# Reordering the small products and one pair of evictions in the first stage of a filtered-convolution and spectral kernel

## The reference

```python
# layer 0: group norm, 2x upsampling FIR in rows and columns, leaky ReLU, 2x downsampling FIR
y = conv(gn(x), up, rows); y = conv(y, up, columns)
y = where(y >= 0, y, 0.01 * y)
y = conv(y, down, rows);   y = conv(y, down, columns)
x = x + y
# layer 1: group norm, 2-D real FFT, a low-rank contraction on 64 x 64 modes (two corners), inverse FFT
x_ft = rfft2(gn(x))
out = contract(x_ft, a, b, c, d)
x = x + irfft2(out)
```

## Time and profile before

| what | us |
|---|---|
| median of 3 runs (lowest to highest) | 4960.16 (4957.18 to 4960.85) |
| the profiled execution | 4952.49 |
| its span, first to last instruction | 4950.7 |
| PE busy in the span | 4650.8 (94%) |
| DVE busy | 3450.2 (70%) |
| ACT busy | 3279.4 (66%) |
| POOL busy | 3176.7 (64%) |
| first and last x1b<-ring on DVE (line 796), of 256 | 47.9 and 2643.5 |

### The profile page before, as it was taken

How to read it: one execution, slowest core, us unless ns; L and a number is a source line. 1 busy time by engine, 2 the same in 40 slices (tenths; PEclk the granted TensorE clock), 3 DMA queues, 4 the chain that set the end, 5 groups by cost and what they waited for, 6 DMA issues and landing times. The chain is left out here.

```text
span 4950.7 us, 244841 instructions
## 1 busy us (share of the span) xinstructions
PE 4650.8 (94%) x102182; PEld 3998.5 (81%) x102182; DVE 3450.2 (70%) x5227; ACT 3279.4 (66%) x5782; POOL 3176.7 (64%) x3334
## 2 busy tenths in 40 slices
PE   7999999999999999999997599999999999999999
PEld 6887888888878888888886477777777777779999
DVE  5776777777777677767776777777777777773333
ACT  6767767767677677677773577777777777762332
POOL 6867858858678588577681477777777777760000
PEclk9999999999999999999998799999999999999999
DMA  2132132231321321322324122222222222229999
GB/s 61 56 103 71 56 112 62 58 116 57 90 85 57 107 67 56 108 65 74 100 58 159 41 83 78 78 85 80 81 75 85 80 85 72 85 68 398 420 421 398
DMA packets 609975, 556.27 MB, mean 112 GB/s; under 512 B 16996, under 2 KB 543332, under 8 KB 592612
## 3 DMA queue, kind: packets, MB, share of 16 engines
q1 hardware_dynamic: 609380, 547.21, 33.5%
HBM read 278.71 MB, written 268.44 MB: 111 GB/s over the span
## 5 line engine op out<-in xcount | busy, mean ns | idle before, releaser
L1328 DVE TENSOR_TENSOR Ml<-ring,Mh 128x1024 f16<-128x1024 f32 x832 | 982.3, 1219 | 331.0 <-ACT Mh L1291 325.4
L1291 ACT ACTIVATE Mh<-ring 128x1024 f16<-128x1024 f32 x832 | 810.9, 1024 | 336.5 <-PE ring L1217 336.2
L269 POOL TENSOR_TENSOR A<-Af,A 128x788 f16<-128x788 f32 x512 | 862.7, 1685 | 41.4
L754 DVE SCALAR_TENSOR_TENSOR Y<-ring,Y 128x532 f16<-128x532 f32 x1024 | 682.2, 706 | 279.5 <-ACT Y L607 278.9
L1217 PE MATMUL ring<-wcur,b_hi 64*128 64x128 f16 x16384 | 737.4, 217 | 43.9 <-POOL wcur L1156 39.2
L607 ACT ACTIVATE Y<-ring 128x532 f16<-128x532 f32 x1024 | 575.1, 610 | 270.1 <-PE ring L369 257.1
L1217 PEld LDWEIGHTS ring<-wcur,b_hi 64*128 64x128 f16 x16384 | 614.8, 94 | 146.8 <-DVE Ml L1328 100.7
L1217 PE MATMUL ring<-wcur,b_lo 64*128 64x128 f16 x8192 | 711.6, 217 | 0.0
L369 PE MATMUL ring<-uth,A 64*128 64x138 f16 x12288 | 605.0, 223 | 62.0 <-issue 29.4
L267 POOL CAST A<-Af 128x788 f16<-128x788 f32 x512 | 429.8, 839 | 273.2 <-ACT Af L585 269.0
L769 DVE TENSOR_TENSOR Z<-ring,Z 128x1024 f16<-128x1024 f32 x256 | 313.5, 1225 | 316.4 <-ACT Z L618 316.4
(11 more groups left out here) (156 smaller groups left out, 10777.6 us busy)
## 6 DMA issues: line engine op xcount, KB each, us to landing
xb<-in_x SPq DMA_DIRECT2D x258, 256.0 KB, 2.9
x<-x1b SPq DMA_DIRECT2D x64, 1024.0 KB, 6.3
spec<-sp_out SPq DMA_DIRECT2D x256, 256.0 KB, 3.5
xin<-spec SPq DMA_DIRECT2D x128, 512.0 KB, 3.6
fd<-ft SPq DMA_DIRECT2D x128, 512.0 KB, 4.0
F<-fd SPq DMA_DIRECT2D x64, 1024.0 KB, 20.0
xq<-x SPq DMA_DIRECT2D x64, 1024.0 KB, 16.8
out<-yq SPq DMA_DIRECT2D x64, 1024.0 KB, 18.5
```

The source lines that it names most:

```text
L269: pool.tensor_tensor(lo, Af[:, n], hi, ALU.subtract).then_inc(e_al, 1)
L754: dve.scalar_tensor_tensor(out=Y[:, e, 1, m], in0=ring[:, pr[u], :, 0:UPS], scalar=0.0, in1=Y[:, e, 0, m], op0=ALU.max, op1=ALU.subtract). ...
L1291: act.activation(hi, ps, ACT.Copy).then_inc(e_hi, 1)
L1328: dve.tensor_tensor(lo, ps, hi, ALU.subtract).then_inc(e_lo, 1)
```

## The change

Three things move; no arithmetic is changed.

1. In `down_rows` the 6 products over the 40 rows of Yt stand first instead of last, right behind `up_rows` (64 rows). `p_s3` is now raised by the last of the 48 products over Y.
2. `tails` is split in two. `tail_up` (At) stays in place and is followed by the transform products. `tail_down` (Yb, Yc) now stands behind the transform products, with the 40-row products of Yc right ahead of `up_cols` (64 rows). It writes to bank 0 of the pair U2, columns 266 to 393, beside image 2's columns 0 to 265, and raises a semaphore of its own, `p_zt`. PE's wait for `e_yl` of image 1 moves ahead of it.
3. ACT's Zt<-ring moves from behind Z<-ring to behind G<-ring, ahead of Y<-ring of image 2, and waits for `p_zt` and for the products of image 2 (they write the same bank). DVE's Zt<-ring moves from behind Yt<-ring to between Y<-ring of image 2 and of image 3.

```diff
             def down_rows(q, o, pr):
+                pe.wait_ge(e_ytl, q)
+                for wt in range(2):
+                    bank = ring[:, pr, wt, :]
+                    pairs(bank.rearrange("p (i h) -> p i h", i=IMGS)[:, :, TL0:H],
+                          lambda v: Yt[:, o, v, 128 * wt:128 * wt + 128],
+                          lambda v: dtailh[:, v, 0:IMGS * TLN], start=True)
                 for m in range(IMGS):
                     pe.wait_ge(e_yl, 4 * (q - 1) + m + 1)
...
-                pe.wait_ge(e_ytl, q)
-                for wt in range(2):
...
                 mm.then_inc(p_s3, 1)
...
+            def tail_up(e, pr):
+                pairs(ring[0:TR, pr, 0, 0:UPS], lambda v: At[:, e, v].rearrange("p i t -> p (i t)"),
+                      lambda v: uth[:, v, 0:UPS], start=True, stop=True).then_inc(p_tl, 1)
+
+            def tail_down(o, pr):
+
+                zt = ring[0:TR, pr, 0, UPS:UPS + H]
+                for t, (lo, hi) in enumerate(((0, LO), (HI0, H))):
+                    pairs(zt[:, lo:hi], lambda v: Yb[:, o, v, t].rearrange("p i t -> p (i t)"),
+                          lambda v: dth[:, v, LO * t:LO * t + hi - lo], start=(t == 0))
+                pairs(zt[:, TL0:H], lambda v: Yc[:, o, v].rearrange("p i t -> p (i t)"),
+                      lambda v: dtailh[:, v, IMGS * TLN:], stop=True).then_inc(p_zt, 1)
...
                 if up:
                     pe.wait_ge(e_yl, 4 * q + 1)
                     pe.wait_ge(e_at, q + 1)
-                if down:
-                    pe.wait_ge(e_yb, 2 * q)
-                    pe.wait_ge(e_yc, q)
-                if up or down:
-                    tails(e, o, pr[TF], up, down)
+                    tail_up(e, pr[TF])
...
                 if up:
+                    pe.wait_ge(e_yl, 4 * q + 2)
+                if down:
+                    pe.wait_ge(e_yb, 2 * q)
+                    pe.wait_ge(e_yc, q)
+                    tail_down(o, pr[U2])
+                if up:
                     pe.wait_ge(e_al, 2 * q + 2)
-                    pe.wait_ge(e_yl, 4 * q + 2)
                     up_cols(q, k, 2, pr[U2], 0)
...
-                    act.wait_ge(p_tl, q + 1)
-                    act.activation(Zt[:, o, 0, :], ring[0:TR, pr[TF], 0, 0:H], ACT.Copy).then_inc(e_zth, 1)
...
+                if down:
+                    act.wait_ge(p_zt, q)
+                    if up:
+                        act.wait_ge(p_s2, 8 * q + 6)
+                    act.activation(Zt[:, o, 0, :], ring[0:TR, pr[U2], 0, UPS:UPS + H], ACT.Copy).then_inc(e_zth, 1)
                 if up:
                     y_high(2, U2)
                     y_high(3, U3)
...
-                if down:
-                    dve.wait_ge(e_zth, q)
-                    dve.tensor_tensor(Zt[:, o, 1, :], ring[0:TR, pr[TF], 0, 0:H], Zt[:, o, 0, :],
-                                      ALU.subtract).then_inc(e_ztl, 1)
                 if stats is not None:
                     x_stats(*stats)
                 if up:
                     y_low(2, U2)
+                if down:
+                    dve.wait_ge(e_zth, q)
+                    dve.tensor_tensor(Zt[:, o, 1, :], ring[0:TR, pr[U2], 0, UPS:UPS + H], Zt[:, o, 0, :],
+                                      ALU.subtract).then_inc(e_ztl, 1)
+                if up:
                     y_low(3, U3)
```

More of the change, by code:

```diff
@@ L150, in phase1 @@
         e_g32, e_gh, e_gl = sem("e_g32"), sem("e_gh"), sem("e_gl")
-        p_s1, p_s2, p_s3, p_tl, p_s4, p_s5, p_s6 = [sem(n) for n in ("p_s1", "p_s2", "p_s3", "p_tl", "p_s4", "p_s5", "p_s6")]
+        p_s1, p_s2, p_s3, p_tl, p_zt, p_s4, p_s5, p_s6 = [sem(n) for n in ("p_s1", "p_s2", "p_s3", "p_tl", "p_zt", "p_s4", "p_s5", "p_s6")]
         p_st, p_st2 = sem("p_st"), sem("p_st2")
@@ L390, in down_rows @@
                         for t, (lo, hi) in enumerate(((0, LO), (HI0, H))):
-                            pairs(ring[:, pr, wt, 128 * m + lo:128 * m + hi],
-                                  lambda v: Y[:, o, v, m, t, 128 * wt:128 * wt + 128],
-                                  lambda v: dth[:, v, LO * t:LO * t + hi - lo], start=(m == 0 and t == 0))
-                pe.wait_ge(e_ytl, q)
-                for wt in range(2):
[L396 to L399, removed]
@@ L400, in down_rows @@
-                mm.then_inc(p_s3, 1)
-            def tails(e, o, pr, up, down):
-                if down:
[L404 to L413, removed]
+                            mm = pairs(ring[:, pr, wt, 128 * m + lo:128 * m + hi],
+                                       lambda v: Y[:, o, v, m, t, 128 * wt:128 * wt + 128],
+                                       lambda v: dth[:, v, LO * t:LO * t + hi - lo], stop=(m == IMGS - 1 and t == 1))
@@ L619, in step @@
                                    ).then_inc(e_zh, 1)
-                    act.wait_ge(p_tl, q + 1)
-                    act.activation(Zt[:, o, 0, :], ring[0:TR, pr[TF], 0, 0:H], ACT.Copy).then_inc(e_zth, 1)
                 if up:
                     act.wait_ge(p_tl, q + 1)
-                    act.activation(Yt[:, e, 0, :], ring[0:TR, pr[TF], 0, H:H + UPS], ACT.Relu).then_inc(e_yth, 1)
+                    act.activation(Yt[:, e, 0, :], ring[0:TR, pr[TF], 0, 0:UPS], ACT.Relu).then_inc(e_yth, 1)
                 if next_half is not None and k % HALF == 2:
@@ L772, in step @@
                     dve.wait_ge(e_yth, q + 1)
-                    dve.scalar_tensor_tensor(out=Yt[:, e, 1, :], in0=ring[0:TR, pr[TF], 0, H:H + UPS], scalar=0.0,
+                    dve.scalar_tensor_tensor(out=Yt[:, e, 1, :], in0=ring[0:TR, pr[TF], 0, 0:UPS], scalar=0.0,
                                              in1=Yt[:, e, 0, :], op0=ALU.max, op1=ALU.subtract).then_inc(e_ytl, 1)
-                if down:
-                    dve.wait_ge(e_zth, q)
-                    dve.tensor_tensor(Zt[:, o, 1, :], ring[0:TR, pr[TF], 0, 0:H], Zt[:, o, 0, :],
-                                      ALU.subtract).then_inc(e_ztl, 1)
                 if stats is not None:
```

## The result

The change makes the kernel slower: 5212.07 us median (5211.08 to 5220.41, 4 runs) against 4960.51 us for the kernel before, a ratio of 1.0512 (95% interval 1.0494 to 1.053). The forecast was 5197 with a range of 5130 to 5245. The profiled execution spans 5210.0 us, 259.3 more than before; the forecast sum was 237.

The account below looks back on a forecast made before the run. PE's own queue was taken to bound the kernel. 192 plain steps at 0.79 us and 63 with scales at 1.35 add 237 us to the profiled 4952.5, giving 5189, as a median 5197; 80% range 5130 to 5245.

Parts of the forecast that it names:

- What bounds the kernel: First stage: in most steps PE's own queue sets the pace, busy 473 of 500 us; other engines have slack.
- The wait that takes the place: At `linear_cols` PE waits about 1.1 us for DVE's low half of Zt, now behind image 2's low half.
- What PE gains: Fewer changes of row count between PE's products: image 2 reached 0.30 to 0.42 us earlier per step, 0.33 taken.
- gone are Y to Yt, Yt to Yb and Yc to At: Three gaps between PE's weight loads vanish in the new order: 0.12 + 0.095 + 0.085 = 0.30 us per step.
- the 0.20 behind the transform products: PE's gap between transform products and the next loads: may stay whole or lose 0.12 us.
- The plain step: Steps without scales, 192 of them: `linear_cols` starts 0.79 us later, held by Zt's low half.
- Z 0.09 earlier: ACT starts Z at 963.67 instead of 963.76, as Y's last product now raises `p_s3`.
- The step with scales: Every fourth step, 63 in all, where ACT makes scales between Yt and g: `linear_cols` starts 1.35 us later.
- The sum: Over 255 steps: 192 x 0.79 + 63 x 1.35 = 237 us more.
- The gain reaches the end: Rival: Zt's low half is not PE's last wait, so only PE's gain remains, 4853 to 4883 us; chance 0.05.
- It costs more: Rival: PE reaches image 2 as late as before, or its clock drops; 5245 to 5330 us; chance 0.07.
- a lower clock: Half of the 5245 to 5330 us rival (chance 0.07): PE's granted clock drops as it stands 1.1 us each step.

Follow-up runs that it names:

- yt_first_only: The kernel before with only the new `down_rows` (Yt's 40-row products first): 4931.68 us against 4954.37, ratio 0.995.
- late_wait: The changed kernel with PE's wait for Zt's low half moved right ahead of the products that read Zt: 4911.52 us, ratio 0.9906 to the kernel before.
- zt_before_image2: The changed kernel with DVE's low half of Zt taken ahead of its low half of image 2: 5050.48 us, ratio 1.0185 to the kernel before.
- before_all128: The kernel before, nothing reordered, with At, Yb and Yc weights held at 128 columns (88 zeros): 4916.34 us against 4954.30, ratio 0.9926.
- late_wait_all128: late_wait with At, Yb and Yc weights held at 128 columns (88 zeros): 4872.56 us, ratio 0.9834 to the kernel before.

## Why the prediction was right, and where it was off

**What bounds the kernel.** Right: PE's own queue set the pace, and a PE gain shows in the time (yt_first_only: 0.11 us a step, 23 us in all).

**The wait that takes the place.** Right, in place and mechanism: the supplier of an unmoved wait was moved behind a longer operation. late_wait shows it by taking the wait off the path, zt_before_image2 by taking one link out of the chain.

**What PE gains: off.** I took 0.33 us to image 2; from the last loads of `up_rows` it is 0.11 (the sums of the table's columns: 0.26 + 3.82 after against 0.386 + 3.80 before). The step that failed is "gone are Y to Yt, Yt to Yb and Yc to At". Only one gap went; Y to Yt came back as Y to At, Yc to At as Yc to image 2, and the 0.20 behind the transform products stayed whole. The rule of the Trainium skill that I used ("TensorEngine Tiling (Array Packing)", Key Properties) speaks of the tiling mode, and the same page's list of configurations (Tiling Modes) names columns beside rows; I had read rows alone. The traces agree with the list: three loads of 40*40 are followed by 64*128 only 0.159 us after the first of them, with 40*128 in their place it is 0.01 (984.32 - 984.31) and the loads mix. All shapes stood in the earlier trace rows.

**The plain step.** Forecast +0.79, measured 4.52 - 3.44 = 1.08 from Z on, less the 0.11 by which Z itself comes earlier: +0.97. The missing 0.2 is the PE gain: image 2 comes later than I had it, and Zt hangs on image 2. PE stood 1.17 us where I had 1.1, but both ends of this stand came some 0.2 later than worked out, so the agreement is luck and checks neither end. "Z 0.09 earlier" was right (0.11).

**The step with scales.** Forecast +1.35. The median of Z to `linear_cols` went from 3.71 to 5.10, so less 0.11 it is +1.28. Image 2's start has no part there, since ACT runs without a break, which is why this term held while the other did not. One of these steps, ACT and DVE after:

```profile
1073.15 0.26 ACT L637 ACTIVATE Zt<-ring 40x128 f16<-40x128 f32 x1
1073.31 1.09 ACT L608 ACTIVATE Y<-ring 128x532 f16<-128x532 f32 x2
```

```profile
1073.94 0.71 DVE L758 SCALAR_TENSOR_TENSOR Y<-ring,Y 128x532 f16<-128x532 f32 x1 [0.91 <-ACT Y L608]
1074.57 0.27 DVE L785 TENSOR_TENSOR Zt<-ring,Zt 40x128 f16<-40x128 f32 x1
```

**The sum.** 192 x 0.97 + 63 x 1.28 = 267 us against a measured 259; I had 237. So the term of the plain steps was 35 us short and the range held, as it allowed for errors of this size. Taken step by step in the two traces, from one start of Z to the next, the 192 plain steps lost 170 us and the 63 with scales 91, together 261, all of the loss. The medians give 186 and 81. The difference in the plain steps lies mostly behind the transform units: six steps, each the second behind such a pass, are 2.3 to 3.3 us shorter than before. Why they are is open.

**The rivals.** "The gain reaches the end" fell as argued: Zt low could not be early. "It costs more" was half true: the ordering helped less than I thought inside the step, for the reason of columns and not for the one I gave. Its other half, a lower clock, is at most a small part. The window of the earlier trace rows was too short to judge by: in the first stage of the kernel before, the trace's clock records have 24 stretches at a granted clock of 0.50, 92 us in all. In the changed kernel it has 33, 126 us in all. At half speed 34 us more cost at most 17 of the 259 (an estimate from these two sums), and yt_first_only stood at 0.50 for 140 us and was faster than the kernel before.

## What to carry to other kernels

When a producer is moved later in its queue, look for waits on it that were not moved with it: a wait that was free at its old place can become the step's last one, and moving it down to the first real reader may be all that is needed. To count what the array loses between small products, compare the full shape of neighbouring weights, rows and columns, and try holding narrow weights at full width before reordering anything: here that alone was worth 0.7%, and with the reordering and the late wait 1.7%.

## What the runs showed of the hardware

- A change of the weights' shape class (in the shapes read here: whether it has 40 or 64 rows or 128, and whether it has 40 columns or 128) cost about 0.12 us of PE's queue between fp16 products (1.574 against 1.455 from Y to At), and about 0.19 from fp16 At to the float32 products (0.447 against 0.256). From the float32 products to fp16 Yb the first load came 0.20 sooner (1.088 against 0.892), but Yc behind it only 0.10 (1.38 against 1.28).
- 40 and 64 rows count as the same class (40*128 and 64*128 loads mix); 40 and 128 columns do not.
- Widening weights from 40 to 128 columns did not make three loads longer (0.23 and 0.24 us for At). Yb's six took 0.23 in before_all128 too, but 0.33 in late_wait_all128, where they stand right behind the float32 products.
- After some of its stands PE's granted clock fell. In a step with scales PE had idled 1.75 us ahead of 1074.91, and its twelve loads took 1.20 us instead of 0.69 at a granted clock of 0.50, the lower of its two levels, 1.2 GHz. Twelve loads of this kind took over 0.8 us in 9 of the changed kernel's 256 groups and in none of late_wait's 256. Five of the nine followed a stand of 3.6 to 4.0 us, four one of 1.75, but 55 steps had a stand of about 1.75, so such a stand was mostly not followed by a fall (columns: window, its us, busy us by engine, PEclk):

```profile
1074.00:1075.00 1.00, 0.06 (x1) 0.09 (x2) 1.00 (x3) 1.00 (x2) 0.92 (x2) 0.96 0.00 0
1075.00:1076.00 1.00, 1.00 (x11) 1.00 (x12) 0.64 (x2) 0.54 (x3) 0.92 (x3) 0.50 0.12 25
1076.00:1078.00 2.00, 2.00 (x38) 1.90 (x38) 0.05 (x1) 0.00 (x0) 1.92 (x3) 0.50 0.00 0
```
